# Four graph layers on one core: the constant numbers that the VectorE compares with are read from PSUM, and the GpSimd clears between groups of gathers are left out

## The reference

```python
h = relu(layernorm(x)); x = x + L0(h)   # per edge type r of 16: h[src] @ weight[r], summed per dst
h = relu(layernorm(x)); x = x + L1(h)   # elu(mean over edges of h[src] @ W_l.T + b_l + h @ W_r.T)
h = relu(layernorm(x)); x = x + L2(h)   # m = silu([h[src], h[dst], edge_attr] @ w1 + b1) @ w2 + b2, summed, then an update MLP
h = relu(layernorm(x)); x = x + L3(h)   # attention: softmax per dst of q[dst].k[src], with 4 rules, 8 edge types
```

## Time and profile before

| | |
|---|---|
| time, median of 3 runs | 2359.71 us (2354.27 to 2363.16) |
| profiled execution: time / span | 2357.4 us / 2355.6 us |
| busy share of the span | PE 65%, PEld 58%, DVE 45%, ACT 21%, POOL 70% |
| mean granted TensorE clock | 0.644 of full |
| gathers of the first layer | from 69.6 us; last ones end at about 589 us |
| of the mean layer | 621 to 1082 us |
| of the message layer | 1133 to 1690 us |
| of the attention layer | 1801 to 2285 us |

### The profile page before, as it was taken

One profiled execution on the slowest core, in us unless ns is written; L12 is line 12 of the kernel. 1 busy time (PEld: TensorE's weight loads), 2 busy tenths in 40 slices (PEclk: granted clock), 3 DMA queues, 4 the chain that ended last, 5 costly groups with the idle time before them and its releaser, 6 DMA issues.

```text
span 2355.6 us, 28036 instructions
## 1 busy us (share of the span) xinstructions
PE 1527.0 (65%) x8443; PEld 1363.2 (58%) x8443; DVE 1062.7 (45%) x2213; ACT 486.8 (21%) x1153; POOL 1660.1 (70%) x1677
## 2 busy tenths in 40 slices
PE   7573333333588888764887777877858656657774
PEld 3243223322488888764777777777745436646673
DVE  6691111111587666643422222222255765455587
ACT  4000000000098676611100000000032121111120
POOL 5777777777388877872677777777517777777760
PEclk9775555555587777765755555555576886656677
DMA  8613131222111111110322232222217322323220
GB/s 280 205 28 94 24 95 32 68 41 50 25 35 40 35 36 39 38 23 10 79 58 57 58 62 59 57 58 57 44 52 254 84 72 80 77 63 86 68 68 14
DMA packets 159863, 159.27 MB, mean 68 GB/s; under 512 B 108361, under 2 KB 111993, under 8 KB 158748
## 3 DMA queue, kind: packets, MB, share of 16 engines
q0 software_dynamic: 48352, 68.42, 13.4%
q1 hardware_dynamic: 111372, 89.07, 13.3%
HBM read 118.71 MB, written 46.06 MB: 70 GB/s over the span
## 4 chain that ended last, share of the span: by engine, by line
POOL 67%; issue 19%; PE 6%; DVE 4%; DMA 4%; SPq 1%; ACT 0%; POOLq 0%; DVEq 0%; ACTq 0%
POOL flat L591 62%; POOL quiet L579 4%; DMA table<-flat 2%; PE ps L1404 1%; PE ps L1357 1%; PE ps L1657 1%; DMA flat<-table,flat 1%; PE ps L1332 1%; PE ps L1341 1%; PE ps L1601 0%; PE ps L1369 0%; DVE var L681 0%; DVE uvT L674 0%; DVE mean L672 0%; PE ps L1527 0%
## 5 line engine op out<-in xcount | busy, mean ns | idle before, releaser
L591 POOL DMA_INDIRECT flat<-table,flat x1061 | 1146.5, 1081 | 405.0 <-issue 289.1
L1404 PE MATMUL ps<-flat,oh 128*128 x1664 | 323.5, 375 | 393.4 <-DMA flat<-table,flat 367.5
L1404 PEld LDWEIGHTS ps<-flat,oh 128*128 128x128 f32 x1664 | 307.1, 285 | 420.0 <-issue 418.2
L801 DVE TENSOR_TENSOR oh<-iota_n,drel 128x1024 f32<-128x1024 f32 x156 | 190.9, 1224 | 624.7 <-PE ps L1404 424.7
L591 POOL DMA_INDIRECT flat<-table,tile_idx x359 | 348.5, 971 | 111.1 <-issue 94.2
L1369 PE MATMUL ps<-msg,oh 128*128 128x64 f32 x832 | 189.1, 421 | 121.2 <-ACT msg L1225 121.2
L1369 PEld LDWEIGHTS ps<-msg,oh 128*128 128x128 f32 x832 | 179.8, 328 | 129.7 <-issue 129.7
L1382 PE MATMUL ps<-uvT,flat 128*128 128x192 bf16 x2200 | 220.9, 271 | 17.2 <-ACT flat L1207 16.9
L1382 PEld LDWEIGHTS ps<-uvT,flat 128*128 128x128 bf16 x2200 | 215.2, 110 | 22.2 <-issue 17.5
L1527 PEld LDWEIGHTS ps<-uvT,ohT 128*128 128x128 f32 x832 | 191.0, 315 | 17.6
L840 DVE TENSOR_TENSOR flat<-flat,iota_node 128x1536 bf16<-128x1536 f32 x110 | 193.3, 1758 | 3.0
(11 more groups left out here) (321 smaller groups left out, 1514.7 us busy)
## 6 DMA issues: line engine op xcount, KB each, us to landing
table<-flat SPq DMA_DIRECT2D x52, 512.0 KB, 4.9
drow<-slot_node SPq DMA_DIRECT2D x104, 256.0 KB, 3.4
flat<-table,flat POOLq DMA_INDIRECT x1061
flat<-edge_attr_by_slot SPq DMA_DIRECT2D x52, 128.0 KB, 3.7
edge_attr_padded<-edge_attr SPq DMA_DIRECT2D x1, 6250.0 KB
flat<-table,tile_idx POOLq DMA_INDIRECT x359
flat<-tile_source SPq DMA_DIRECT2D x22, 256.0 KB, 3.3
edge_attr_by_slot<-flat SPq DMA_DIRECT2D x2, 2048.0 KB, 6.7
```

Source lines behind the costliest of these rows:

```text
L591: nc.gpsimd.indirect_dma_start(dest(t % PLACES), None, table, at_).then_inc(tile_gat[k % TRING], 16)
L801: V.tensor_tensor(oh[:, b], iota_n[:].unsqueeze(1).broadcast_to([P, SG, P]), drel[:, g * SG:(g + 1) * SG].unsqueeze(2).broadcast_to([P, SG ...
L1404: last = T.matmul(acc[:, bass.ds(n[j] * pitch + shift, width)], oh[:, b % 2, j, :], got[:, bass.ds(place[j], width)], start=False, stop=Tr ...
```

## The change

The numbers that DVE compares with are copied into PSUM by TensorE (a matmul with the identity), and the compares read them there: `onehots` in the first layer from group `OWN` = 14 on, in the mean layer and in the message layer; `sources` in the mean layer; `onehots_T` in the message layer, where a `tensor_scalar` with a number per partition becomes a `tensor_tensor` with that number broadcast from PSUM. The attention layer's compares are not changed. To have room, the picked rows have one PSUM buffer in place of two, and so have the transposed edge attributes of the message layer (`tp[0]` alone). `breath` and all its 168 calls are gone.

```diff
-        picked_ps = [aux[:, 1024 * q:1024 * q + 256 * PICK].rearrange("p (k c) -> p k c", k=PICK)[:, :, 0:3 * D].rearrange("p k (a d) -> p k a d", a=3)
-                     for q in range(2)]
+        picked_ps = aux[:, 0:256 * PICK].rearrange("p (k c) -> p k c", k=PICK)[:, :, 0:3 * D].rearrange("p k (a d) -> p k a d", a=3)
+        assert 256 * PICK <= 1024
+        columns_ps = (ps[:, 2560:2560 + P], aux[:, 1024:1024 + P])
+        nodes_ps = aux[:, 1024 + P:1024 + P + NT]
+        spare2 = tp[1]
+        OWN = WHOLE[0] + 2
...
-            breaths = [0]
-
-            def breath():
-                breaths[0] += 1
-                nc.gpsimd.memset(quiet[:], 0.0).then_inc(s("breath"), 1)
-                pool.wait_ge(s("breath"), breaths[0])
...
-                if g:
-                    breath()
                 if g >= TRING:
                     pool.wait_ge(s("used"), g - TRING + 3 + 3)
                 gather_tiles(0, g, table0_d.rearrange("n (r d) -> (n r) d", d=D), lambda p: got0[:, p, 0:D], tile_idx0)
...
-            def onehots(g, b):
-
-                V.tensor_tensor(oh[:, b], iota_n[:].unsqueeze(1).broadcast_to([P, SG, P]), drel[:, g * SG:(g + 1) * SG].unsqueeze(2).broadcast_to([P, SG, P]),
+            def onehots(g, b, columns=iota_n):
+
+                V.tensor_tensor(oh[:, b], columns[:].unsqueeze(1).broadcast_to([P, SG, P]), drel[:, g * SG:(g + 1) * SG].unsqueeze(2).broadcast_to([P, SG, P]),
                                 ALU.is_equal).then_inc(s("oh"), 1)
...
-                V.tensor_scalar(ohT[:, b], drow[:, b], iota_p[:, 0:1], None, ALU.is_equal).then_inc(s("ohT"), 1)
+                if k == 0:
+                    V.tensor_tensor(ohT[:, b], drow[:, b], spare2[:, P:P + 1].unsqueeze(2).broadcast_to([P, SG, P]), ALU.is_equal).then_inc(s("ohT"), 1)
+                else:
+                    V.tensor_scalar(ohT[:, b], drow[:, b], iota_p[:, 0:1], None, ALU.is_equal).then_inc(s("ohT"), 1)
...
                     V.tensor_tensor(src_oh[:, m % BINS, 0:ON_DVE, :], src_row[:, b].unsqueeze(1).broadcast_to([P, ON_DVE, PICK * P]),
-                                    iota_node[:, CH * c:CH * c + ON_DVE].unsqueeze(2).broadcast_to([P, ON_DVE, PICK * P]), ALU.is_equal).then_inc(s("src_oh"), 1)
+                                    nodes_ps[:, CH * c:CH * c + ON_DVE].unsqueeze(2).broadcast_to([P, ON_DVE, PICK * P]), ALU.is_equal).then_inc(s("src_oh"), 1)
...
-            def pick(q, b):
-
-                pe.wait_ge(s("picked"), q + 1)
+            def pick(q):
+
+                pe.wait_ge(s("picked"), q + 2)
...
+                    if l == 0 and g == WHOLE[0]:
+                        pe.wait_ge(s("ahead_read"), 4 * WHOLE[0] + 1)
+                        T.matmul(columns_ps[0], ident[:], iota_n[:], start=True, stop=True).then_inc(s("numbers"), 1)
...
+            T.matmul(columns_ps[1], ident[:], iota_n[:], start=True, stop=True)
+            T.matmul(nodes_ps, ident[:], iota_node[:], start=True, stop=True).then_inc(s("numbers"), 1)
...
-                    pe.wait_ge(s("eaT_sb"), g + 1)
+                    pe.wait_ge(s("eaT_sb"), g + 2)
                     ea_T(g + 2, b + 2)
...
+            T.matmul(spare2[:, 0:P], ident[:], iota_n[:], start=True, stop=True)
+            T.matmul(spare2[:, P:P + 1], ident[:], iota_p[:], start=True, stop=True).then_inc(s("numbers"), 1)
             ea_T(0, 0)
+            pe.wait_ge(s("eaT_sb"), 1)
             ea_T(1, 1)
```

More of the change, by code:

```diff
@@ L242, in network @@
         drop = sb("drop", [1, 1])
-        quiet = sb("quiet", [P, 500], bf16)
         drop_b = sb("drop_b", [P, 1])
@@ L610, in _ @@
             for g in range(TG):
-                if g and g % 2 == 0:
-                    breath()
                 if g >= TRING:
@@ L631, in _ @@
                     pool.wait_ge(s("key_parts"), 1)
-                if k:
-                    breath()
                 if k >= TRING:
@@ L829, in first_layer @@
                     dve.wait_ge(s("used"), g + 1)
-                    onehots(g, g % 2)
+                    if g == OWN:
+                        dve.wait_ge(s("numbers"), 1)
+                    onehots(g, g % 2, columns_ps[0] if g >= OWN else iota_n)
                     if g + 1 < WHOLE[0]:
@@ L840, in sources, with picked @@
                     V.tensor_tensor(src_oh[:, m % BINS, 0:ON_DVE, :], src_row[:, b].unsqueeze(1).broadcast_to([P, ON_DVE, PICK * P]),
-                                    iota_node[:, CH * c:CH * c + ON_DVE].unsqueeze(2).broadcast_to([P, ON_DVE, PICK * P]), ALU.is_equal).then_inc(s("src_oh"), 1)
+                                    nodes_ps[:, CH * c:CH * c + ON_DVE].unsqueeze(2).broadcast_to([P, ON_DVE, PICK * P]), ALU.is_equal).then_inc(s("src_oh"), 1)
                     dve.wait_ge(s("src_oh"), TN // CH * q + c + 1)
-            def picked(q, b):
+            def picked(q):
                 dve.wait_ge(s("src_used"), BINS + TN // CH * (q + 1))
                 first = ((q + 1) * 2 * SG + 2 * SG - PICK) % PLACES
-                V.tensor_reduce(got0[:, first:first + PICK, 0:D], picked_ps[b].rearrange("p k a d -> p k d a"), AX, ALU.add).then_inc(s("picked"), 1)
+                V.tensor_reduce(got0[:, first:first + PICK, 0:D], picked_ps.rearrange("p k a d -> p k d a"), AX, ALU.add).then_inc(s("picked"), 1)
             def mean_layer():
+                dve.wait_ge(s("numbers"), 2)
                 for i in range(G // 2):
@@ L855, in mean_layer @@
                     dve.wait_ge(s("used"), G + 2 * i + 1)
-                    onehots(2 * i, 0)
+                    onehots(2 * i, 0, columns_ps[1])
                     if q < PICKS:
-                        picked(q, q % 2)
+                        picked(q)
                     dve.wait_ge(s("used"), G + 2 * i + 2)
-                    onehots(2 * i + 1, 1)
+                    onehots(2 * i + 1, 1, columns_ps[1])
             segment_bounds()
@@ L965, in before2 @@
                 dve.wait_ge(s("used"), 2 * G + g + 1)
-                onehots(g, b)
+                onehots(g, b, spare2[:, 0:P])
             def step2(g, b, left):
@@ L979, in _ @@
             dve.sem_inc(s("edge_sum"), 1)
+            dve.wait_ge(s("numbers"), 3)
             before2(0, 0)
@@ L1218, in take_ea @@
                 act.wait_ge(s("eb_ps"), g + 1)
-                A.copy(eaT[:, b % 2], tp[b % 2][:, 0:2 * P].rearrange("p (q k) -> p q k", q=2)).then_inc(s("eaT_sb"), 1)
+                A.copy(eaT[:, b % 2], tp[0][:, 0:2 * P].rearrange("p (q k) -> p q k", q=2)).then_inc(s("eaT_sb"), 1)
             def step2(g, b, left):
@@ L1381, in pick @@
                         for j in range(PICK):
-                            last = T.matmul(picked_ps[b][:, j], src_oh[:, m % BINS, k, j * P:(j + 1) * P], h_parts[:, :, t, :],
+                            last = T.matmul(picked_ps[:, j], src_oh[:, m % BINS, k, j * P:(j + 1) * P], h_parts[:, :, t, :],
                                             start=(t == 0 and j % 2 == 0), stop=(t == TN - 1), skip_group_check=True)
@@ L1390, in step @@
                     if l == 1 and g % 2 == 0 and g // 2 < PICKS:
-                        pick(g // 2, g // 2 % 2)
+                        pick(g // 2)
                     if l == 0 and g + 1 < WHOLE[0]:
                         typed0(g + 1)
+                    if l == 0 and g == WHOLE[0]:
+                        pe.wait_ge(s("ahead_read"), 4 * WHOLE[0] + 1)
+                        T.matmul(columns_ps[0], ident[:], iota_n[:], start=True, stop=True).then_inc(s("numbers"), 1)
                     n = slot_tiles(PE_, g)
@@ L1517, in ea_T @@
                 for q in range(2):
-                    last = T.transpose(tp[b % 2][:, q * P:(q + 1) * P], ea[:, b % 2, q * P:(q + 1) * P], ident[:])
+                    last = T.transpose(tp[0][:, q * P:(q + 1) * P], ea[:, b % 2, q * P:(q + 1) * P], ident[:])
                 last.then_inc(s("eaT_ps"), 1)
```

## The result

The changed kernel takes 2139.2 us (median of 4 runs, 2135.15 to 2142.9) against 2361.4 us of the kernel before (median of 4): a ratio of 0.906, with a 95% interval of 0.904 to 0.909. The forecast was 2148. The profiled execution takes 2141.09 us with a span of 2139.3, so 216.3 us of span have gone.

A forecast was written before the change was run, and what follows sets the result against it. GpSimd's stream of gathers was taken as the bound: 128 us of stalls plus 87 of clears minus 5 given back, 210 off the profiled 2357.4, gives 2147, stated as 2148 for the median; range 2130 to 2200 at 0.8.

The forecast's parts named there:

- GpSimd's stream of gathers sets the end: All four gathering stretches, 1860 of 2356 us: GpSimd's gathers themselves are the bound, not what is done with them.
- Stalls 128 us: Gathers stalled under the changed compares become plain: 22 us in the first layer, 65 in the mean, 41 in the message.
- Clears 87 us: All four layers: dropping the 168 clears saves 0.50 us each, 0.56 in the attention layer, 87 us in all.
- That the two add up: Whole kernel: 128 us of stalls and 87 us of clears were summed as separate gains.
- Compares as long from PSUM, the transposed one 0.48 us longer, at no cost: DVE's compares keep their length; the message layer's transposed one goes from 747 ns to about 1225, cost 0.
- TensorE at 15.2 us a pair, 5 us given back: Mean layer: TensorE's pair of groups takes 0.2 us more than GpSimd's 15.0, so 22 pairs give back 5 us.
- the sum that I had set beside mine: Mean layer by the clock rule: TensorE at 13.0 us a pair, nothing given back, the sum 5 us larger.
- The message layer fits: Message layer: TensorE has 9.3 us of work in a 10.0 us cycle per group, 0.7 us to spare.
- Rival 1: TensorE becomes the bound in the mean, perhaps the message layer: 2181, or 2205 with both; chance 0.17.
- rival 3: The clears did something: without them each gather costs more, 60 ns more eating the 87 us: 2235; chance 0.07.
- rival 2: A broadcast operand in PSUM leaves the stalls, so only the clears count: 2270; chance 0.06.
- rival 4: Slower: DVE's broadcast read from PSUM is slow, about 2400 at 2.3 times the compare time; chance 0.03, other losses included.

The follow-up runs named there:

- e7: The changed kernel with half the gathers left out in the mean and the message layer: 1878.7 us, ratio 0.795 to the kernel before.
- e1: The changed kernel with its 168 clears put back, compares still reading from PSUM: 2227.5 us, ratio 0.943 to the kernel before.
- e6: The changed kernel with the message layer's transposed compare a tensor_scalar from SBUF again: 2148.8 us, ratio 0.910 to the kernel before.

## Why the prediction was right, and where not

- **GpSimd's stream of gathers sets the end**: right. The chain still says so, and in the table of gathers above GpSimd waited for a consumer for 0.3 us in all (and 3.8 us for the attention layer's table). e7 adds that with half the gathers the message layer is 234 us shorter and the mean layer 30.
- **Stalls 128 us**: right as a sum for the whole change. 22, 65 and 41 were forecast; the first layer lost 46.9 - 24 = 23, the mean layer 77.9 - 12 = 66, the message layer 68.2 - 24 = 44: 133 us.
- **Clears 87 us**: right. With the compares in PSUM they cost 88 (e1).
- **That the two add up** was silently assumed when I laid the stalls to the compares alone. It holds only in the order "compares first". The clears alone gave 132 us, the PSUM reads alone (e1) 137, both 222: 47 us of stalls go with either. The sum came out right because the whole change takes both away; had only the clears been left out, the same working would have been wrong by 45 us.
- **Compares as long from PSUM, the transposed one 0.48 us longer, at no cost**: right (0.46 us; it ends well ahead of the sum).
- **TensorE at 15.2 us a pair, 5 us given back**: the one term that failed, with a small price. The timeline of PE in the changed kernel has these picks at the start of the mean layer:

```profile
622.97 10.54 PE L1377 MATMUL ps<-uvT,flat 128*128 128x192 bf16 x100
...
638.21 9.77 PE L1377 MATMUL ps<-uvT,flat 128*128 128x192 bf16 x100
...
653.26 10.75 PE L1377 MATMUL ps<-uvT,flat 128*128 128x192 bf16 x100
...
668.42 10.02 PE L1377 MATMUL ps<-uvT,flat 128*128 128x192 bf16 x100
```

  A pair took 15.2, 15.1 and 15.2 us at first. That was not its pace "over long": the 22 reductions of the picked rows (L841) start from 617.5 to 917.2 us, 14.3 us apart in the mean, below the 15.0 us of the gathers, at a granted clock of 0.91 (the window 750 to 850 above). Where TensorE was slower, at first, the ring took it up: GpSimd waited for TensorE for 0.3 us in the whole layer, and 0 was given back. That is the sum that I had set beside mine from the rule of the Trainium skill's page "TensorE: Matmul & The Clock Gate", Part 1 on the HAM clock gate, but the trace agrees with the rule in part only: the clock rose, yet not to 1.00, and the pair took 14.3 us, not 13.0.
- **The message layer fits**: right, with 0.85 us to spare for the 0.7 forecast. My 9.3 us counted 0.2 us twice, since the next group's transposes start before the sum has ended; the work is 10.0 - 0.85 = 9.1 us. But the margin is no measure of the bound, as e7 shows.
- The attention layer gave 25.8 of 27. Together 219 - 3 us between the stretches = 216, for 210 forecast: the stretches gave 4 us more than the 215 of the sum (the stalls 5 more, the attention layer 1 less), 5 were not given back, and 3 were lost between the stretches. The other 3 of the 9 us between 2148 and 2139 are the step from the profiled execution to the median, which was upwards in the forecast and is 1.9 us downwards here.

Rival 1 and rival 3 fell with the profile after; rival 2 with the gathers at 0.94 us; rival 4 with the 1222 ns. Of rival 3 something was true in the other direction: beside compares from SBUF the clears did something, they made stalls.

What stays open: why a stalled gather ends 0.82 us behind the compare and not sooner, and why a gather holds up a DVE operation only in a part of its run. No run here looked into a gather. Nor was it tried which of the two SBUF inputs must move to PSUM.

## What to carry to other kernels

Where GpSimd issues the gathers that bound a kernel, look at the gathers' median and most in the profile: where there is a second price beside the plain one, see in the timeline whether a DVE operation runs when a dear gather begins. Move one input of long DVE operations with two SBUF inputs to PSUM (a constant costs one matmul), the long back-to-back ones first; short single ones may be out of the way already, by their place. Before adding up two gains, ask whether one changes the place of the other's instructions: here a pause of 0.5 us decided over 0.7 us of stall in each group of the message layer (1056 against 972 ns, 8 gathers).

## What was not expected of the hardware

- A gather that begins while a DVE operation with two SBUF inputs runs ends 0.80 to 0.82 us behind that operation, wherever in it it began, as long as more than 0.12 us of it were left (0.39, 0.26, 0.93, 1.01 us in: 0.82, 0.81, 0.81, 0.80; 0.81 to 0.83 for all 204 such gathers of over 1 us in the kernel before); one that began 0.24 us ahead of it takes its plain 0.94 us. A `tensor_scalar` from SBUF does the same (0.79 us), and when it begins 0.48 to 0.70 us into a gather it is held up itself, to 1.46 us behind the gather's start (e6).
- A clear of 500 bf16 columns on GpSimd takes 0.53 us, one of 1400 takes 1.28 us: by these two, an estimate of 0.12 us and 0.83 ns a column.
- TensorE's work for a group of the message layer takes 9.1 us at a granted clock of 0.53 (10.0 less 0.85 of waiting) and 4.8 us at 1.00 (5.2 less 0.39, e7); it got the lower level with all the gathers and the higher one with half of them.
